# A four-block hybrid layer on one core: value rows repeated by TensorE into PSUM, and the update made there

## The chip, the cores and the metric

One core of a Trainium2 chip runs the program. The metric is the device time of one execution in microseconds (us). Names of engines: PE is TensorE (PEld its weight loads), DVE is VectorE, ACT is ScalarE, POOL is GpSimd, SP is SyncE, which only issues transfers here.

## The reference

2,048 tokens of 128 features pass through four sublayers, each with a layer norm in front and a residual behind: a gated delta attention (the one that the change touches), a mixture of 8 experts with top-2 routing, a random-feature attention, and the same mixture of experts again. The first sublayer, with 16 heads of 8 features, is:

```
q, k = l2norm(x @ Wq), l2norm(x @ Wk);  v = x @ Wv;  beta = sigmoid(x @ Wbeta)
def step(state, (qt, kt, vt, bt)):                    # over 2,048 tokens
    state = state * (1 - bt * kt kt^T) + bt * (vt kt^T)     # 8x8 per head
    return state, einsum('bhij,bhj->bhi', state, qt)
out = layernorm(outs) * ln_g + ln_b
out = (out * silu(x @ Wg)) @ Wout
```

The product with `kk` is element by element, so each of the 16 x 8 x 8 entries of the state is a scalar recurrence of its own along the tokens: state = decay * state + fresh, with decay = 1 - beta k_i k_j and fresh = beta v_i k_j.

## The kernel before, in words

Tokens are worked in four blocks of 512 (`NB`, index `c`). The recurrence has 1,024 scalar rows, which are 8 tiles of 128 partitions (`HD`, index `i`): partition (h, j) of tile i holds entry i, j of head h. So there are 32 steps, n = 8c + i, and each is one `tensor_tensor_scan` of 128 x 512 on DVE (L794), which starts from the last column of the same tile in the block before.

The operands of step n are made in these places. The k of a block (`kT`, L771) is stored to DRAM (`k_rows`, L301) and read back eight times, each time with row i of every head repeated over its 8 partitions (`spread`, L307) into `decay[:, i]`; v (`vT`, copied from PSUM by ACT, L524) goes through `v_rows` into `fresh[:, i]` in the same way (L299, L308). POOL multiplies `decay` by `bkT` = beta * k (`decay_product`, L424), ACT makes it 1 - decay (`one_minus`, L548), DVE multiplies `fresh` by `bkT` (`update`, L786) and scans. POOL then multiplies the state by q (`read_product`, L433), and PE sums over j (`sum_heads`).

Beside the steps, passes of the neighbouring blocks are spread over the loop: projections of q, k, v (`project_qk`, `project_v`), ACT's squares and raw copies (`square`), the sums of squares by PE (`sum_squares`), their square roots (`norms`), reciprocals (`clamp`), ACT's widening (`widen`) and PE's transposes (`expand`) that bring the reciprocal norms to the place of k and q, `unit_k` and `unit_q`; then, for the block behind, `copy_oT`, `turn_o`, `stats_o`, `ln_scale`, `normalise_o`, `turn_n`, `affine_nT`, `open_gates`, `out_a`, `add_a`, the next layer norm (`ln_rows`, `turn_rows`), and the routing of the first mixture (`logits`, `choose`, `rank`, `locate`, and the scatters of POOL, L442).

The order is written out by hand: each engine has a loop over n with `if i == ...` in it, and every instruction waits for semaphores that others raise. Each engine runs its own list strictly in order, so what stands behind a waiting instruction waits too. In the kernel before PE has no instruction that belongs to a single step except the head sums, so its loop can run ahead of DVE's. PSUM has eight banks of 512 float32 columns, `ps[:, 0..7, :]`: 0 to 2 hold q, k and v, 3 and 4 the sums of squares and the widened norms, 5 transposes, logits and ranks, 6 head sums, 7 transposes and the output product. Ahead of the loop come the layer norm of x, the projections of block 0, and for all four blocks beta (sigmoid) and the gate (silu).

The orders that the change touches, on PE and on DVE:

```
for n in range(NSTEP + HD + 2):      # DVE
    if n + 1 < NSTEP: update(n + 1)
    if n < NSTEP: scan(n)
    ...                              # choose, locate, stats_o, unit_k, open_gates, ... by i
```

Of the kernel before, what the change touches and what calls it, by code (L numbers as in the profile page):

```python
# [22 lines left out]
P = 128  # L23
# [3 lines left out]
H = 16  # L27
# [40 lines left out]
def program(nc, x, Wq, Wk, Wv, Wbeta, Wg, Wout, ln_g, ln_b, W_qkv, proj, W_out, b_out, w_g, c_fc, c_proj, out):  # L68
# [8 lines left out]
    with ctx:  # L77
# [51 lines left out]
        v_rows = nc.dram_tensor("v_rows", [NB, P, BK], F32).ap()  # L129

        with ExitStack() as a:
# [17 lines left out]
            vT = sb("vT", [P, 2, BK], F32, a)  # L149
# [3 lines left out]
            fresh = sb("fresh", [P, HD, BK], F32, a)  # L153
# [4 lines left out]
            nT = sb("nT", [P, BK], F32, a)  # L158
# [3 lines left out]
        with ExitStack() as mb:  # L162
# [110 lines left out]
        def _(sp):  # L273
# [23 lines left out]
            for c in range(NB):  # L297
                sp.wait_ge(v_ready, c + 1)
                sp.dma_start(v_rows[c], vT[:, c % 2, :]).then_inc(v_out, 16)  # L299
                sp.wait_ge(k_ready, c + 1)  # L300
                sp.dma_start(k_rows[c], kT[:, c % 2, :]).then_inc(k_out, 16)  # L301
                sp.wait_ge(v_out, 16 * (c + 1))
                sp.wait_ge(k_out, 16 * (c + 1))
                for i in range(HD):
# [3 lines left out]
                    sp.dma_start(fresh[:, i, :], spread(v_rows, c, i)).then_inc(fresh_in[i], 16)  # L308
# [68 lines left out]
        def _(pool):  # L377
# [10 lines left out]
            pool.memset(base_share[:], 0.0)  # L388
            pool.memset(later_tile[:], 1.0).then_inc(const_made, 1)
# [9 lines left out]
            for by_head in heads:  # L399
# [6 lines left out]
                               pattern=[[-1, P]], channel_multiplier=1)  # L406
            for e in range(NE):
# [41 lines left out]
            for n in range(NSTEP):  # L449
# [5 lines left out]
                if c >= 2 and i >= 2:  # L455
# [5 lines left out]
            read_product(NSTEP - 1)  # L461

# [40 lines left out]
        def _(act):  # L503
# [115 lines left out]
            ln_root(0, 0)  # L619
            turned_x(0, 5)  # L620
# [16 lines left out]
            one_minus(0)  # L637
            one_minus(1)
            for n in range(NSTEP + HD):
# [107 lines left out]
        def _(dve):  # L747
# [29 lines left out]
            def unit_q(c):  # L777
# [740 lines left out]
```

## Time and profile before

| | |
|---|---|
| median of 3 runs | 610.31 us (609.3 to 611.79) |
| profiled execution | 608.01 us |
| its span, first to last instruction | 606.1 us |
| mean granted TensorE clock | 0.766 of 2.4 GHz |
| busy: PE, DVE, ACT, POOL | 377.2, 330.3, 235.6, 268.1 us |

The profile is of one execution. Busy time is the sum of the durations of an engine's instructions, whether they ran freely or were held up while running. The granted clock is 1.00 at 2.4 GHz and 0.50 at 1.2 GHz; a value between is a mean over a stretch with both.

### The profile page before, as it was taken

The numbers are of one execution on the slowest core, as the hardware profiler recorded it, in microseconds if no ns is written. First come the engines' busy times: TensorE is split into PE (matmuls) and PEld (weight loads), VectorE is DVE, ScalarE is ACT, GpSimd is POOL, SyncE is SP. The second block draws the span as 40 slices with busy tenths as digits, with TensorE's granted clock in tenths as the row PEclk, the third lists the DMA queues.
The fourth block names the chain that finished last, engine by engine and source line by source line (L and its number), as shares of the span: only waits on it lengthen the run. The fifth ranks groups of instructions, "written<-read, shape, count | busy, mean of one in ns | idle before, by whom it ended". The sixth has DMA issues, their size and how long they took to land.

```text
span 606.1 us, 6487 instructions
## 1 busy us (share of the span) xinstructions
PE 377.2 (62%) x2106; PEld 247.0 (41%) x2106; DVE 330.3 (54%) x718; ACT 235.6 (39%) x343; POOL 268.1 (44%) x286
## 2 busy tenths in 40 slices
PE   4654628234154219999906899977776209999920
PEld 1422415112032107888803533333334207888720
DVE  4379797999984301231129699976776501111105
ACT  2472525223223203332303699877656301322300
POOL 3076886687875392564532200000523550545540
PEclk9796556765555559999956999996887557999965
DMA  4382959179102320212032433440000120122016
GB/s 113 100 229 78 315 180 340 67 256 316 38 26 44 149 74 27 76 52 68 33 105 74 104 93 96 100 145 1 32 14 27 35 77 24 52 74 73 28 57 176
DMA packets 46657, 60.14 MB, mean 99 GB/s; under 512 B 6816, under 2 KB 24864, under 8 KB 46624
## 3 DMA queue, kind: packets, MB, share of 16 engines
q1 hardware_dynamic: 41440, 51.09, 28.8%
q0 software_dynamic: 4608, 8.44, 4.1%
q8 instruction: 17, 0.28, 0.2%
q10 hardware_dynamic: 576, 0.21, 0.1%
q14 instruction: 16, 0.13, 0.1%
HBM read 34.46 MB, written 20.00 MB: 90 GB/s over the span
## 4 chain that ended last, share of the span: by engine, by line
PE 41%; DVE 25%; issue 7%; ACT 5%; DMA 4%; POOL 3%; SPq 1%; POOLq 0%; DVEq 0%; ACTq 0%
PE ps L1116 37%; DVE state L794 5%; DVE fresh L786 3%; DVE feat L1041 3%; POOL slots_x L442 2%; PE ps L1234 2%; ACT expo L698 2%; DVE ranked L845 2%; DVE xres L990 1%; DVE xres L985 1%; PE ps L1194 1%; DMA got<-chosen_y 1%; DMA xe<-slots_x 1%; ACT L698 1%; DMA slots_x<-rows_x,put_at 1%
## 5 line engine op out<-in xcount | busy, mean ns | idle before, releaser
L442 POOL DMA_INDIRECT slots_x<-rows_x,put_at x64 | 69.0, 1078 | 149.5 <-DVE put_at L874 130.6
L486 POOL DMA_INDIRECT chosen_y<-ye,y_to x80 | 79.3, 991 | 94.4 <-DVE ye L976 65.0
L610 ACT ACTIVATE hT<-ps 128x640 f32<-128x640 f32 x64 | 45.1, 704 | 139.4 <-PE ps L1116 133.8
L1041 DVE SCALAR_TENSOR_TENSOR feat<-expo,ps 128x1024 f32<-128x1024 f32 x64 | 76.8, 1218 | 11.5 <-ACT expo L698 11.1
L1116 PE MATMUL ps<-xeT,cfc_sb 128*128 128x320 f32 x256 | 75.7, 451 | 1.8 <-DVE xeT L958 1.8
L698 ACT ACTIVATE expo<-ps,minus_one 128x1024 f32<-128x1024 f32 x64 | 70.2, 1114 | 11.9 <-PE ps L1116 8.0
L1116 PE MATMUL ps<-cproj_sb,hT 128*128 128x128 f32 x640 | 74.6, 275 | 0.3
L1116 PEld LDWEIGHTS ps<-cproj_sb,hT 128*128 128x128 f32 x640 | 73.0, 192 | 0.9 <-issue 0.6
L958 DVE COPY xeT<-ps 128x640 f32<-128x640 f32 x16 | 13.2, 825 | 98.5 <-PE ps L1234 98.5
L424 POOL TENSOR_TENSOR decay<-decay,bkT 128x512 f32<-128x512 f32 x32 | 52.2, 1631 | 32.0 <-DMA decay<-k_rows 32.0
L794 DVE TENSOR_TENSOR_SCAN state<-decay,state,fresh 128x512 f32<-128x512 f32 x32 | 58.1, 1816 | 1.7 <-ACT decay L548 1.7
L1116 PEld LDWEIGHTS ps<-xeT,cfc_sb 128*128 128x128 f32 x256 | 47.7, 199 | 24.0 <-ACT hT L610 6.8
L433 POOL TENSOR_TENSOR read<-state,qT 128x512 f32<-128x512 f32 x32 | 44.6, 1394 | 20.6 <-DVE state L794 15.7
L976 DVE COPY ye<-ps 128x640 f32<-128x640 f32 x16 | 13.2, 825 | 63.4 <-PE ps L1116 63.4
L786 DVE TENSOR_TENSOR fresh<-fresh,bkT 128x512 f32<-128x512 f32 x32 | 34.9, 1091 | 7.8 <-DMA fresh<-v_rows 7.6
L1234 PE MATMUL ps<-ident,xe 128*128 128x128 f32 x80 | 12.5, 292 | 35.6 <-DMA xe<-slots_x 35.6
L570 ACT ACTIVATE std<-mv,eps_col 128x4 f32<-128x4 f32 x17 | 5.0, 296 | 70.3 <-DVE mv L828 26.9
L1116 PE MATMUL ps<-stk,pstk 97*128 97x512 f32 x64 | 24.2, 468 | 8.9 <-DVE feat L1041 8.0
L548 ACT ACTIVATE decay<-decay 128x512 f32<-128x512 f32 x32 | 19.8, 626 | 24.7 <-POOL decay L424 24.7
L1182 PE MATMUL ps<-ident,otok 128*128 128x128 f32 x16 | 4.5, 434 | 37.5 <-ACT otok L559 37.5
L1234 PEld LDWEIGHTS ps<-ident,xe 128*128 128x128 f32 x80 | 10.4, 151 | 38.6 <-issue 35.7
L1116 PE MATMUL ps<-feat,kvl 128*32 128x512 f32 x128 | 20.2, 707 | 8.3 <-DVE feat L1041 8.3
(188 smaller groups left out, 596.5 us busy)
## 6 DMA issues: line engine op xcount, KB each, us to landing
decay<-k_rows SPq DMA_DIRECT2D x32, 256.0 KB, 5.7
fresh<-v_rows SPq DMA_DIRECT2D x32, 256.0 KB, 6.8
stk<-part SPq DMA_DIRECT2D x96, 64.0 KB, 2.0
slots_x<-empty_rows SPq DMA_DIRECT2D x16, 322.5 KB, 8.0
xe<-slots_x SPq DMA_DIRECT2D x16, 322.5 KB
cfc_sb<-in_L_ffn_c_fc SPq DMA_DIRECT2D x2, 2048.0 KB, 8.7
got<-chosen_y SPq DMA_DIRECT2D x16, 256.0 KB, 4.7
chosen_y<-empty_rows SPq DMA_DIRECT2D x8, 256.0 KB
```

The lines of the kernel that those rows point to most:

```text
L424: pool.tensor_tensor(decay[:, i, :], decay[:, i, :], bkT[:, c % 2, :], ALU.mult).then_inc(product_ready, 1)
L433: pool.tensor_tensor(read[:, i, :], state[:, i, :], qT[:, c % 2, :], ALU.mult).then_inc(read_ready, 1)
L442: pool.indirect_dma_start(out=slots_x[k], out_offset=bass.IndirectOffsetOnAxis(ap=put_at[:, c, kk, t:t + 1], axis=0), in_=rows_x[:, kk * N ...
L486: pool.indirect_dma_start(out=chosen_y, out_offset=bass.IndirectOffsetOnAxis(ap=y_to[:, b, i:i + 1], axis=0), in_=ye[:, b, i * D:(i + 1) * ...
L548: act.activation(decay[:, n % HD, :], decay[:, n % HD, :], ACT.Identity, scale=-1.0, bias=1.0).then_inc(decay_ready, 1)
L610: act.activation(hT[:, b, f, :].rearrange("p (a n) -> p a n", a=2), ps[:, 2 + 2 * (f % 2):4 + 2 * (f % 2), 0:HALF], ACT.Gelu).then_inc(h_r ...
L698: act.activation(expo[:, g % 3, :], flat(ps[:, pair, :]), ACT.Exp, bias=minus_one[:]).then_inc(f_exp, 1)
L786: dve.tensor_tensor(fresh[:, i, :], fresh[:, i, :], bkT[:, c % 2, :], ALU.mult).then_inc(update_ready, 1)
L794: dve.tensor_tensor_scan(out=state[:, i, :], data0=decay[:, i, :], data1=fresh[:, i, :], initial=state[:, i, BK - 1:BK], op0=ALU.mult, op1 ...
L1041: dve.scalar_tensor_tensor(out=feat[:, g % 4, :], in0=expo[:, g % 3, :], scalar=1.0, in1=flat(ps[:, pair, :]), op0=ALU.min, op1=ALU.max).t ...
L1116: return pe.matmul(o, lhsT, rhs, start=start, stop=stop, **kw)
L1234: ins = pe.transpose(ps[:, i // TB, (i % TB) * P:(i % TB + 1) * P], xe[:, b, i, 0:D], ident[:])
```

## The change

The value rows no longer pass through DRAM. ACT copies v to `vhi` as float32r, DVE puts the rest into `vlo`, and for each step PE multiplies both by a selection matrix `sel[:, i]` (row i of each head, repeated over 8 partitions) into PSUM bank 3 or 4 by turns (`repeat_v`). `update` and the scan work on that bank. The sums of squares move to bank 7, the widened norms to banks 0 and 1. The scratch of `choose` in this stage, and the result of `affine_nT`, lie in bank 5. The gates and the betas of blocks 2 and 3 move from ahead of the loop into its first steps, and block 1's own preparation moves by one to two steps. On POOL the last two scatters of the loop go behind the last `read_product`.

```diff
-                sp.wait_ge(v_ready, c + 1)
-                sp.dma_start(v_rows[c], vT[:, c % 2, :]).then_inc(v_out, 16)
...
-                    sp.dma_start(fresh[:, i, :], spread(v_rows, c, i)).then_inc(fresh_in[i], 16)
...
+            pool.memset(sel_f[:], 0.0)
...
+            pool.affine_select(out=sel_f[:].rearrange("p i (h j) -> p i h j", j=HD),
...
-                if c >= 2 and i >= 2:
+                if c >= 2 and i >= 2 and n + 1 < NSTEP:
...
             read_product(NSTEP - 1)
+            for j in (6, 7):
+                scatter(0, 1, j)
...
-                copy(vT[:, c % 2, :], ps[:, 2, :]).then_inc(v_ready, 1)
+                copy(vhi[:, c % 2, :], ps[:, 2, :]).then_inc(vhi_ready, 1)
...
-                act.activation(nT[:], ps[:, 5, :], ACT.Identity, scale=lng[:], bias=lnb[:]).then_inc(nT_ready, 1)
+                act.activation(ps[:, 5, :], ps[:, 5, :], ACT.Identity, scale=lng[:], bias=lnb[:]).then_inc(nT_ready, 1)
...
+            ln_root(0, 0)
+            turned_x(0, 5)
             act.wait_ge(wall_in, 16 * 4)
...
-            turned_x(1, 7)
             norms(0)
+            turned_x(1, 5)
             widen(0)
             open_beta(0, 6)
-            turned_x(2, 5)
-            turned_x(3, 7)
-            for c in range(1, NB):
-                open_beta(c, (6, 5, 7)[c - 1])
+            open_beta(1, 6)
             act.wait_ge(w_in, 16 * 6)
-            for c in range(NB):
-                open_gate(c, (6, 5, 7, 6)[c])
...
                 if n + 2 < NSTEP:
                     one_minus(n + 2)
-                if i == 0 and c == 0:
+                if n == 0:
+                    turned_x(2, 5)
+                    turned_x(3, 6)
+                    open_beta(2, 5)
+                    open_beta(3, 6)
+                if n == 1:
+                    open_gate(0, 5)
+                    open_gate(1, 6)
+                if n == 2:
+                    open_gate(2, 5)
+                    open_gate(3, 6)
                     square(1)
+                if n == 3:
+                    copy_v(1)
+                    norms(1)
+                if n == 4:
+                    widen(1)
...
+            def low_v(c):
+                dve.wait_ge(vhi_ready, c + 1)
+                dve.tensor_tensor(vlo[:, c % 2, :], ps[:, 2, :], vhi[:, c % 2, :].bitcast(F32),
+                                  ALU.subtract).then_inc(vlo_ready, 1)
...
-                dve.tensor_tensor(fresh[:, i, :], fresh[:, i, :], bkT[:, c % 2, :], ALU.mult).then_inc(update_ready, 1)
+                c = n // HD
+                dve.wait_ge(vrep_ready, n + 1)
+                dve.tensor_tensor(ps[:, 3 + n % 2, :], ps[:, 3 + n % 2, :], bkT[:, c % 2, :],
+                                  ALU.mult).then_inc(update_ready, 1)
...
-                dve.tensor_tensor_scan(out=state[:, i, :], data0=decay[:, i, :], data1=fresh[:, i, :],
+                dve.tensor_tensor_scan(out=state[:, i, :], data0=decay[:, i, :], data1=ps[:, 3 + n % 2, :],
...
+            dve.wait_ge(sel_made, 1)
+            dve.tensor_copy(sel[:], sel_f[:]).then_inc(sel_made, 1)
+            low_v(0)
             clamp(0)
...
-                if i == 2 and c == 0:
+                if n == 4:
+                    low_v(1)
                     clamp(1)
+                if i == 1 and 1 <= c < NB - 1:
+                    low_v(c + 1)
...
-                if i == 3 + (c == 0) and c + 1 < NB:
+                if i == 3 + 2 * (c == 0) and c + 1 < NB:
                     unit_k(c + 1)
...
-                if i == 4 + (c == 0) and c + 1 < NB:
+                if i == 4 + 2 * (c == 0) and c + 1 < NB:
                     unit_q(c + 1)
...
             def project_qk(c):
                 if c:
-                    pe.wait_ge(raw_ready, c)
+                    pe.wait_ge(k_ready, c)
+                    pe.wait_ge(q_ready, c)
...
+            def repeat_v(n):
+                c, i = divmod(n, HD)
+                if i == 0:
+                    pe.wait_ge(vlo_ready, c + 1)
+                if n >= 2:
+                    pe.wait_ge(scan_done, n - 1)
+                mm(ps[:, 3 + n % 2, :], sel[:, i, :], vhi[:, c % 2, :], stop=False)
+                mm(ps[:, 3 + n % 2, :], sel[:, i, :], vlo[:, c % 2, :], start=False).then_inc(vrep_ready, 1)
...
             project_qk(0)
+            project_v(0)
+            sum_squares(0)
             pe.wait_ge(wbeta_ready, 1)
             project_beta(0, 6)
-            project_v(0)
-            turn_x(1, 7)
-            sum_squares(0)
+            turn_x(1, 5)
             expand(0)
+            pe.wait_ge(beta_ready, 1)
+            project_beta(1, 6)
+            pe.wait_ge(sel_made, 2)
+            repeat_v(0)
             turn_x(2, 5)
...
             for n in range(NSTEP + HD + 2):
                 c, i = divmod(n, HD)
-                if i == 0 and c == 0:
+                if n + 1 < NSTEP:
+                    repeat_v(n + 1)
+                if n == 0:
+                    project_beta(2, 5)
+                    project_beta(3, 6)
+                if n == 1:
+                    pe.wait_ge(w_in, 16 * 6)
+                    for j in range(2):
+                        pe.wait_ge(beta_ready, 3 + j)
+                        project_gate(j, 5 + j)
+                if n == 2:
+                    for j in range(2):
+                        pe.wait_ge(gate_ready, 1 + j)
+                        project_gate(2 + j, 5 + j)
                     project_qk(1)
+                if n == 3:
                     project_v(1)
+                    sum_squares(1)
+                if n == 4:
+                    expand(1)
...
                 if i == 1 and c >= 2:
-                    pe.wait_ge(logit_used, c - 1)
+                    pe.wait_ge(chosen_ready, c - 1)
                     rank(0, c - 2, 5)
```

## Rows read from the trace of the kernel before

**Rows 1.** Windows view: stretch, length; busy PE, PEld, DVE, ACT, POOL; clock, DMA share, GB/s.
```profile
71.00:108.00 37.00, 20.63 (x78) 12.41 (x74) 33.67 (x48) 14.51 (x28) 28.65 (x18) 0.60 0.84 274
108.00:146.00 38.00, 11.35 (x60) 6.17 (x52) 37.35 (x61) 9.90 (x21) 30.35 (x23) 0.63 0.61 194
146.00:183.00 37.00, 13.65 (x66) 6.94 (x61) 33.71 (x67) 9.68 (x20) 26.59 (x21) 0.50 0.24 70
```

**Rows 2.** Costliest groups of the page: line, engine, operation, busy us, mean ns, idle before.
```profile
L442 POOL DMA_INDIRECT slots_x<-rows_x,put_at x64 | 69.0, 1078 | 149.5 <-DVE put_at L874 130.6
...
L794 DVE TENSOR_TENSOR_SCAN state<-decay,state,fresh 128x512 f32<-128x512 f32 x32 | 58.1, 1816 | 1.7 <-ACT decay L548 1.7
...
L786 DVE TENSOR_TENSOR fresh<-fresh,bkT 128x512 f32<-128x512 f32 x32 | 34.9, 1091 | 7.8 <-DMA fresh<-v_rows 7.6
```

**Rows 3.** Timeline of DVE: start, duration, instruction, and idle time before it.
```profile
35.86 1.28 DVE L794 TENSOR_TENSOR_SCAN state<-decay,state,fresh 128x512 f32<-128x512 f32 x1 [1.70 <-ACT decay L548]
...
68.71 2.29 DVE L794 TENSOR_TENSOR_SCAN state<-decay,state,fresh 128x512 f32<-128x512 f32 x1
...
103.94 0.63 DVE L786 TENSOR_TENSOR fresh<-fresh,bkT 128x512 f32<-128x512 f32 x1
104.49 1.27 DVE L794 TENSOR_TENSOR_SCAN state<-decay,state,fresh 128x512 f32<-128x512 f32 x1
...
141.51 1.27 DVE L794 TENSOR_TENSOR_SCAN state<-decay,state,fresh 128x512 f32<-128x512 f32 x1
...
173.79 0.16 DVE L835 SCALAR_TENSOR_TENSOR shift<-mv,rstd 128x4 f32<-128x4 f32 x1
```

**Rows 4.** Timeline of all engines, DVE and POOL side by side in block 0.
```profile
39.84 2.18 POOL L424 TENSOR_TENSOR decay<-decay,bkT 128x512 f32<-128x512 f32 x1
40.88 1.68 DVE L786 TENSOR_TENSOR fresh<-fresh,bkT 128x512 f32<-128x512 f32 x1
...
41.98 1.71 POOL L433 TENSOR_TENSOR read<-state,qT 128x512 f32<-128x512 f32 x1
...
42.49 2.28 DVE L794 TENSOR_TENSOR_SCAN state<-decay,state,fresh 128x512 f32<-128x512 f32 x1
```

**Rows 5.** Timeline of all engines, ahead of the scanned stage.
```profile
7.01 0.31 ACT L504 ACTIVATE wbeta<-wall 128x128 f32<-128x128 f32 x1 [2.56 <-DMA wall<-in_L_attn_a_Wbeta]
...
21.43 0.69 DVE L771 TENSOR_TENSOR kT<-raw,ps 128x512 f32<-128x512 f32 x1 [1.41 <-PE ps L1157]
...
28.05 1.26 POOL L424 TENSOR_TENSOR decay<-decay,bkT 128x512 f32<-128x512 f32 x1 [22.39 <-DMA decay<-k_rows]
```

**Rows 6.** Source view of two DVE lines: duration in ns, min/median/max.
```profile
L771 DVE TENSOR_TENSOR kT<-raw,ps x4: 656/678/689, 21.4 to 121.2; 128x512 f32<-128x512 f32 x4
...
L845 DVE TENSOR_TENSOR ranked<-ranked,low_first x16: 191/192/5450, 106.1 to 480.0; 128x32 f32<-128x32 f32 x16
```

**Rows 7.** Timeline of PE, pairs of float32r matmuls in the attention that follows.
```profile
405.36 0.73 PE L1116 MATMUL ps<-stk,pstk 97*128 97x512 f32 x2 [0.41 <-DVE feat L1041]
...
420.89 1.20 PE L1116 MATMUL ps<-stk,pstk 97*128 97x512 f32 x2
```

**Rows 8.** Windows view, around the second of these pairs.
```profile
415.00:420.00 5.00, 4.50 (x18) 2.28 (x19) 3.65 (x7) 4.38 (x8) 0.00 (x0) 0.50 0.00 0
```

**Rows 9.** Timelines of ACT and PE, passes of block 1.
```profile
82.55 1.64 ACT L559 ACTIVATE otok<-ps,shift,rstd 128x128 f32<-128x128 f32 x4 [3.04 <-DVE shift L835]
...
84.24 1.12 PE L1182 MATMUL ps<-ident,otok 128*128 128x128 f32 x4 [10.16 <-ACT otok L559]
87.79 2.07 PE L1116 MATMUL ps<-wout,gated 128*128 128x128 f32 x8 [2.44 <-DVE gated L808]
...
99.03 3.44 PE L1116 MATMUL ps<-head_of,squares 128*128 128x16 f32 x16
```

**Rows 10.** Timeline of DVE, two more instructions.
```profile
52.52 0.66 DVE L771 TENSOR_TENSOR kT<-raw,ps 128x512 f32<-128x512 f32 x1
...
179.21 1.11 DVE L845 TENSOR_TENSOR ranked<-ranked,low_first 128x32 f32<-128x32 f32 x1
```

More of the change, by code:

```diff
@@ L148, in program @@
             kT = sb("kT", [P, 2, BK], F32, a)
-            vT = sb("vT", [P, 2, BK], F32, a)
+            vhi = sb("vhi", [P, 2, BK], F32R, a)
+            vlo = sb("vlo", [P, 2, BK], F32R, a)
+            sel_f = sb("sel_f", [P, HD, P], F32, a)
+            sel = sb("sel", [P, HD, P], F32R, a)
             qT = sb("qT", [P, 2, BK], F32, a)
@@ L770, in unit_k @@
                 dve.wait_ge(rep_mm, 2 * c + 1)
-                dve.tensor_tensor(kT[:, c % 2, :], raw[:, 1, :], ps[:, 3, :], ALU.mult).then_inc(k_ready, 1)
+                dve.tensor_tensor(kT[:, c % 2, :], raw[:, 1, :], ps[:, 0, :], ALU.mult).then_inc(k_ready, 1)
                 dve.wait_ge(k_ready, c + 1)
@@ L836, in ln_scale, with choose @@
                                          op0=ALU.mult, op1=ALU.mult).then_inc(ln_shift[n], 1)
-            def choose(k, c, lg):
+            def choose(k, c, lg, ranked, lg2):
                 wide = lambda ap: ap.unsqueeze(2).broadcast_to((P, TB, NE))
@@ L917, in _ @@
             update(0)
+            dve.wait_ge(ids_made, 1)
             begin_counts(0)
+            small = lambda n: ps[:, 5, 2 * P * (n > 0) + TB * NE * n:2 * P * (n > 0) + TB * NE * (n + 1)].rearrange(
+                "p (t e) -> p t e", e=NE)
             for n in range(NSTEP + HD + 2):
@@ L925, in _ @@
                 if i == 0 and c >= 2:
-                    choose(0, c - 2, ps[:, 5, 0:TB * NE].rearrange("p (t e) -> p t e", e=NE))
+                    choose(0, c - 2, small(0), small(1), small(2))
                 if i == 1 and c >= 2:
@@ L1095, in _ @@
                 elif n in ROUTE_AT:
-                    choose(1, ROUTE_AT[n], logits_in(pair_of(n).start + 1))
+                    choose(1, ROUTE_AT[n], logits_in(pair_of(n).start + 1), ranked[:], lg2[:])
                 elif n in RANK_AT:
@@ L1099, in _ @@
             divide(NB - 1, 1)
-            choose(1, NB - 2, logits_in(1))
+            choose(1, NB - 2, logits_in(1), ranked[:], lg2[:])
             add_b(NB - 1, 3)
@@ L1104, in _ @@
             ln_scale(4, NB - 1)
-            choose(1, NB - 1, logits_in(1))
+            choose(1, NB - 1, logits_in(1), ranked[:], lg2[:])
             locate(1, NB - 1, ranks_in(4))
@@ L1143, in sum_squares @@
                 pe.wait_ge(sq_ready, c + 1)
-                if c:
-                    pe.wait_ge(k_ready, c)
+                if c == 2:
+                    pe.wait_ge(wT_ready, 4)
+                if c >= 3:
+                    pe.wait_ge(xres_a, c - 2)
                 for t in range(TB):
                     for n in range(2):
-                        ins = mm(ps[:, 3, (2 * t + n) * H:(2 * t + n + 1) * H], squares[:, n, t * P:(t + 1) * P], head_of[:])
+                        ins = mm(ps[:, 7, (2 * t + n) * H:(2 * t + n + 1) * H], squares[:, n, t * P:(t + 1) * P], head_of[:])
                 ins.then_inc(sumsq_mm, 1)
             def expand(c):
-                for n, bank in ((1, 3), (0, 4)):
+                pe.wait_ge(raw_ready, c + 1)
+                for n, bank in ((1, 0), (0, 1)):
                     pe.wait_ge(wide_ready, 2 * c + 2 - n)
-                    if n == 0 and c:
-                        pe.wait_ge(q_ready, c)
                     for t in range(TB):
@@ L1297, in _ @@
                     expand(c + 1)
-                if i == 1 and c == 0:
-                    sum_squares(1)
                 if i == 1 and 1 <= c <= NB:
@@ L1306, in _ @@
                     if c == 1:
-                        pe.wait_ge(gate_ready, NB)
                         pe.wait_ge(wT_ready, 4)
                     turn_o(c - 1)
-                if i == 3 and c == 0:
-                    expand(1)
                 if i == 3 and c:
```

66 lines of the change are left out of this document (23 added, 43 removed).

## The prediction

> **What bounds the kernel now.** I read the page first, then the busy time by stage, then the timeline of each engine. The change touches only the scanned stage, from about 36 us to 183 us of a 606.1 us span. In the three windows that hold blocks 1 to 3, DVE is busy 33.67 of 37, 37.35 of 38 and 33.71 of 37 us, POOL 26.6 to 30.4 us, while PE is busy 0.30 to 0.56 of the time at a granted clock of 0.60, 0.63 and 0.50 [rows 1]. So DVE bounds these blocks.
>
> It is busy because it is slowed. 32 scans take 58.1 us, 1816 ns each, and 32 updates 34.9 us, 1091 ns each [rows 2]; alone a scan takes 1.27 us and an update 0.63 us [rows 3]. The difference is 58.1 - 32 x 1.27 = 17.5 us and 34.9 - 32 x 0.63 = 14.7 us. The timeline shows the cause: with a POOL product beside them an update takes 1.68 and a scan 2.28 us, and the POOL products 2.18 and 1.71 us instead of 1.26 [rows 4, 5]. The reader should see that all four have two SBUF inputs. kT<-raw,ps has one SBUF and one PSUM input, and its four executions, some beside POOL, all lie between 0.656 and 0.689 us [rows 6]. One tiny routing instruction with two SBUF inputs takes 0.191 us at best and 5.45 at worst [rows 6].
>
> **The change part by part.** I count from scan start to scan start: block 0 is 35.86 to 68.71, block 1 to 104.49, block 2 to 141.51, block 3 to the shift instruction at 173.79 [rows 3].
>
> *Contention removed.* Update gets PSUM in and out with one SBUF input, scan loses one SBUF input. By kT's row, I take 0.66 for an update and 1.28 for a scan beside POOL; PSUM as output and the scan's PSUM input are not shown, and bounds are the alone values 0.63 and 1.27 below and the stretched 1.68 and 2.28 above, where I take the row nearest in shape, kT's. POOL's products fall to 1.26. If nothing else came in, 32 us would go from DVE. The Trainium skill (SBUF — State Buffer, Who interferes with whom) says that a DVE instruction with at most one SBUF input doesn't contend with GpSimd. It would count the scan as free too, which no row here shows, since the scan also reads its starting value from SBUF.
>
> *A new wait in each step.* repeat_v(n+1) stands at the head of PE's loop n and waits for scan(n-1), because there are two banks; DVE's loop n begins with update(n+1), ahead of scan(n). So DVE's own next update waits for PE each time. The two float32r matmuls are not in the trace; the nearest are the pairs of 512-column fp32r matmuls of the key features, 0.73 us and, at a granted clock of 0.50, 1.20 us [rows 7, 8]. A bare step is scan 1.28 + pair + update 0.60 and about 0.1 of handing over: 2.7 us at 2.4 GHz and 3.2 us at 1.2 GHz, against 3.8 us for a fully stretched pair today (1.61 + 2.20, the starts in rows 4). That alone is a gain of 0.6 to 1.1 us a step.
>
> *What is queued in front of it.* PE works in order, and each repeat_v stands behind the PE work of the loop before. Today these passes wait with nobody behind them but later passes. Now DVE waits behind them:
> loop 3 of a block: turn_n waits for ACT's normalise (1.64), then 1.12, then the pair 1.20 [rows 7, 9]: 4.0 us behind ln_scale, of which kT and bkT cover 1.5: 2.5 us idle.
> loop 4: out_a 2.07 [rows 9] plus the pair, 3.3 us behind open_gates, unit_q covers 0.7: 2.6.
> loop 1: sum_heads, ACT's copy and turn_o, about 3.7 us beside scan and (blocks 2, 3) locate: 1 to 2.
> loop 0 in blocks 1 and 2: project_v and expand (eight transposes, 2 x 1.12): 1 to 2.
> loop 6: turn_rows behind ln_rows (four activations, as the 1.64 of rows 9), in block 1 also behind project_qk and square, since PE can no longer run ahead to start them: 3 to 5.
> loop 7 in block 1: sum_squares, 3.44 at the lower clock [rows 9], and logits before the next pair: 3.
>
> Walking the queues with these durations gives, scan start to scan start. Block 1 at the lower clock throughout: 4.4 + 4.9 + 3.2 + 6.4 + 5.9 + 3.6 + 8.0 + 6.5 = 42.9 us against 35.8. At the higher clock throughout, the pairs save 8 x 0.47 and the listed passes about half of their 16 us, 11.8 in all: 31.1. The dense stretches (expand to turn_o, out_a to project_qk) should run partly at 2.4 GHz; I take half of the difference, 37.1: **+1.3**. Block 2 has no project_qk, square, sum_squares or clamp; choose, thirteen small instructions that take an estimated 2.9 us unstretched, and locate lie under the PE waits: 4.8 + 4.1 + 3.2 + 6.4 + 5.9 + 3.7 + 5.6 + 3.1 = 36.8 at the lower clock, 35.6 mixed, against 37.0: **-1.4**. Block 3 drops project_v, expand and the unit steps: 29.2, mixed 28.5, to the shift, against 32.3: **-3.8**. Its choose also no longer catches stretches such as the 5.45 us.
>
> *Block 0.* turned_x(0) no longer waits behind the weights' arrival, which ACT met at 7.01 [rows 5]; ln_root could run at 5.2, so the front moves by 2.0 us, and sum_squares ahead of project_beta and turn_x(1) gives 0.6 more. kT(0) moves from 21.43 to 18.8, the first decay product from 28.05 to 25.45 [rows 5], and with the gates out of the way scan(0) starts at 25.45 + 1.26 + 0.63 = 27.4 instead of 35.86, 8.4 us sooner. The memset, select and copy that make sel lie before 13 us, where POOL's next product is at 25 us and DVE waits for ACT: nothing; uncovered, an estimated 1 us each. Then it is given back. repeat_v(2) stands behind project_beta(2) and (3), and these behind ACT's turned_x(2) and (3), themselves behind one_minus(2), 30.5: the pair ends about 35.4 and scan(1) starts at 36.1. repeat_v(3) comes behind two gates, repeat_v(4) behind two gates and project_qk(1) (42.4), repeat_v(5) behind sum_squares(1) (45.8), repeat_v(6) behind expand(1), which waits for clamp(1) in DVE's own queue (about 53). So scan(5) starts about 54 and kT(1) about 55.3, later than today's 52.52 [rows 10]. Rows of k go through DRAM as before: kT's end to product is 28.05 - 22.12 = 5.9 us [rows 5]. decay(8), one_minus(8), the wT copies, square(2), sum_squares(2), clamp(2) then follow one another on ACT, PE and DVE as today: scan(8) at 69.8 to 71.4 against 68.71. **+1.9**.
>
> *Removed DMAs.* 32 transfers of fresh and 4 stores go. Only decay transfers feed the first block now, but landing is no longer what the chain waits for after scan(0). Gain in the sum nothing; cover is the PE order above. Without that cover it is up to 1.6 us per early step.
>
> *Tail.* read_product(31) goes ahead of two scatters; but the DVE chain choose, locate, stats_o ends as late as the head sums, so only the routing instruction that took 1.11 instead of 0.19 [rows 6, 10] goes: **-0.9**. rank now waits for chosen_ready: 0.2 at most, behind choose.
>
> The PSUM operand of 64 DVE instructions: kT's median 0.678 against 0.63 of an update would be 0.05 x 64 = 3 us. I take nothing beyond the 0.66 used, since most of it overlaps in the starts. The Trainium skill (VectorE: DVE Perf Modes, The TRN2 errata) gives 120 cycles fixed for PSUM sources and 58 for SBUF; by that the 64 instructions would cost 4.1 us more and the sum would end on the other side of zero.
>
> **Sum.** +1.9 + 1.3 - 1.4 - 3.8 - 0.9 = -2.9 us. The profiled execution took 608.01 us (span 606.1), 2.3 below the median 610.31; -2.9 on it is 605.1, on the median **607.4 us**. Half a per cent, 3.05 us, is about what this kernel's measurement tells from no change.
>
> **Rivals.**
> A, as summed, PE's order eats what contention gives back: 607.4, own range 602 to 613, chance 0.45.
> B, the pairs keep TensorE at 2.4 GHz through most of the blocks. Block 1 -4, block 2 -4, block 3 -6, block 0 +1, tail -1: 596. For it: PE becomes busier. Against: the granted clock is 0.50 to 0.63 today [rows 1], and gaps of 1 to 2 us remain. 0.20.
> C, the other side: TensorE stays at 1.2 GHz through the blocks. +2.7 + 7.1 - 0.2 - 3.1 - 0.9, with 0.2 per step of handing over in the bound steps of block 1: about +7, 617. It decides from a mean clock of about 0.6 in block 1 downward. 0.17.
> D, the scan stays stretched by POOL because its starting value comes from SBUF: 1.0 us on half of the scans, +16: 621. Against: nothing in the rows, which is why it has 0.07.
> E, the waits are shorter than walked and POOL bounds: 32 x 2 x 1.23 = 79 us of products and 16 scatters of 1.08 plus gaps [rows 2], about 100 us instead of 138: 575. For it: all 32 us of stretch. Against: the PE order. 0.06.
> F, the fixed cost of PSUM operands, 3 us by kT's row: 610.4, no change. 0.05. This is the rule of VectorE: DVE Perf Modes in the Trainium skill.
>
> Faster by over 0.5%: half of A, B, E: 0.48. Within: the middle of A and F: 0.26. Slower: the rest of A, C, D: 0.26. The range 594 to 618 holds A, C and most of B, leaves out E and D.
>
> **What would show it.** Right: scans at 1.28 with POOL products at 1.26 throughout; before update, DVE idle ended by PE in nearly every step; scan(0) at 27 to 28 and scan(8) at 69 to 72; a long idle ahead of update(2). Wrong: kT(1) before 52 us; DVE idle before updates under 0.5 us a step (E); scans of 2.28 (D); granted clock over 0.85 or at 0.50 in all blocks (B, C).

## The result, and the profile after

The changed kernel takes 620.07 us (median of 4, 617.86 to 621.44), the kernel before 609.8 (608.9 to 611.79) beside it: 1.016 times as long, 95% interval 1.0121 to 1.02. It is slower by 10 us; 607.4, and at most 618, was forecast. The profiled execution took 620.1 us, its span 618.0 against 606.1.

What was to come off came off. The costliest groups of the page after:

```profile
L442 POOL DMA_INDIRECT slots_x<-rows_x,put_at x64 | 63.0, 985 | 152.1 <-DVE put_at L886 127.6
...
L433 POOL TENSOR_TENSOR read<-state,qT 128x512 f32<-128x512 f32 x32 | 40.7, 1272 | 45.4 <-DVE state L806 39.8
...
L424 POOL TENSOR_TENSOR decay<-decay,bkT 128x512 f32<-128x512 f32 x32 | 40.5, 1267 | 34.4 <-DMA decay<-k_rows 34.4
...
L797 DVE TENSOR_TENSOR ps<-ps,bkT 128x512 f32<-128x512 f32 x32 | 22.2, 694 | 44.7 <-PE ps L1137 44.5
L806 DVE TENSOR_TENSOR_SCAN state<-decay,state,ps 128x512 f32<-128x512 f32 x32 | 40.6, 1270 | 1.6 <-ACT decay L550 1.6
...
L1137 PE MATMUL ps<-vhi,sel 128*128 128x512 f32 x32 | 23.1, 722 | 15.4 <-DVE state L806 15.3
```

Against [rows 2], a scan fell from 1816 to 1270 ns and an update from 1091 to 694: 58.1 + 34.9 - 40.6 - 22.2 = 30.2 us of VectorE gone. The last column of the update's row says where they went: 44.7 us of idle time of VectorE ahead of the updates, 44.5 of it ended by TensorE. Windows of blocks 1 to 3, columns as in [rows 1]:

```profile
74.00:111.00 37.00, 23.00 (x91) 14.87 (x91) 25.92 (x46) 14.97 (x30) 19.96 (x16) 0.68 0.47 149
111.00:150.00 39.00, 19.03 (x78) 10.34 (x76) 28.74 (x63) 11.12 (x23) 25.95 (x23) 0.63 0.37 113
150.00:184.00 34.00, 14.63 (x52) 6.81 (x52) 26.36 (x58) 6.20 (x13) 21.92 (x19) 0.60 0.31 91
```

No engine is full in them: DVE is down to 70 to 78%, TensorE at 43 to 62% at a granted clock of 0.60 to 0.68, a little above that of before. When every engine has time to spare, the stage is bound by what waits for what; e1 below shows how much of that is order.

The timeline of DVE after, answering to [rows 3, 10]:

```profile
5.81 2.91 DVE L764 TENSOR_SCALAR xn<-xres,mv,rstd 128x128 f32<-128x128 f32 x4
...
29.77 1.28 DVE L806 TENSOR_TENSOR_SCAN state<-decay,state,ps 128x512 f32<-128x512 f32 x1 [1.62 <-ACT decay L550]
37.19 0.70 DVE L797 TENSOR_TENSOR ps<-ps,bkT 128x512 f32<-128x512 f32 x1 [6.14 <-PE ps L1137]
37.80 1.27 DVE L806 TENSOR_TENSOR_SCAN state<-decay,state,ps 128x512 f32<-128x512 f32 x1
...
56.68 0.66 DVE L777 TENSOR_TENSOR kT<-raw,ps 128x512 f32<-128x512 f32 x1
```

The same stations for all kernels, read from the same view (starts in us, of the profiled execution; e1 to e10 are the experiments below; shift is the last `shift<-mv,rstd` of the stage, behind scan(30)):

| kernel | scan(0) | kT(1) | scan(8) | scan(16) | scan(24) | shift | span | median, ratio to before |
|---|---|---|---|---|---|---|---|---|
| before | 35.86 | 52.52 | 68.71 | 104.49 | 141.51 | 173.79 | 606.1 | |
| after | 29.77 | 56.68 | 73.98 | 110.80 | 150.34 | 182.52 | 618.0 | 620.07, 1.016 |
| e1 | 29.34 | 50.49 | 66.52 | 102.71 | 136.56 | 169.81 | 602.8 | 604.26, 0.9913 |
| e2 | 28.94 | 54.93 | 71.89 | 108.04 | 143.06 | 172.00 | 605.5 | 608.13, 0.9984 |
| e3 | 34.84 | 49.64 | 65.64 | 102.71 | 142.23 | 174.40 | 610.1 | 612.21, 1.0043 |
| e4 | 30.83 | 52.59 | 68.81 | 105.88 | 142.89 | 175.15 | 607.7 | 610.52, 1.002 |
| e5 | 33.51 | 49.06 | 65.15 | 101.39 | 134.03 | 167.06 | 601.9 | 603.85, 0.9914 |
| e6 | 27.18 | 54.12 | 71.10 | 108.53 | 148.07 | 180.27 | 617.7 | 617.54, 1.0137 |
| e7 | 28.73 | 49.73 | 65.66 | 99.71 | 132.33 | 162.48 | 595.7 | 599.05, 0.9858 |
| e8 | 32.00 | 47.55 | 63.88 | 98.07 | 130.39 | 160.56 | 592.8 | 596.31, 0.9815 |
| e9 | 27.54 | 48.64 | 57.25 | 92.11 | 128.94 | 159.09 | 594.2 | 594.87, 0.9761 |
| e10 | 26.76 | 48.22 | 57.28 | 90.38 | 125.80 | 153.63 | 589.8 | 591.61, 0.9712 |

The changed kernel against the one before, in us: block 0 +5.3 by scan(8), block 1 +1.0, block 2 +2.5, block 3 -0.1, and +3.2 behind the shift.

### The profile page after: what moved, and what is told of

It reads as the page before. It is cut to its first block, busy times and chain, and to the rows that moved or that the text cites. A ratio compares the mean times of both kernels' runs of the same rounds, so it can differ in the third digit from the quotient of the medians.

```text
span 618.0 us, 6592 instructions
## 1 busy us (share of the span) xinstructions
PE 402.2 (65%) x2170; PEld 260.4 (42%) x2170; DVE 303.9 (49%) x723; ACT 235.0 (38%) x343; POOL 249.6 (40%) x288
## 4 chain that ended last, share of the span: by engine, by line
PE 51%; DVE 22%; issue 9%; DMA 6%; ACT 6%; POOL 4%; SPq 1%; POOLq 0%; DVEq 0%; ACTq 0%
PE ps L1137 45%; DVE state L806 4%; DVE feat L1062 3%; POOL slots_x L442 2%; DVE shift L847 2%; PE ps L1268 2%; DMA decay<-k_rows 1%; PE ps L1228 1%; ACT expo L704 1%; DVE xres L1011 1%; DVE xres L1006 1%; DMA got<-chosen_y 1%; ACT otok L561 1%; DMA xe<-slots_x 1%; DVE stats L837 1%
## 5 line engine op out<-in xcount | busy, mean ns | idle before, releaser
L442 POOL DMA_INDIRECT slots_x<-rows_x,put_at x64 | 63.0, 985 | 152.1 <-DVE put_at L886 127.6
L979 DVE COPY xeT<-ps 128x640 f32<-128x640 f32 x16 | 13.2, 824 | 99.1 <-PE ps L1268 99.1
L433 POOL TENSOR_TENSOR read<-state,qT 128x512 f32<-128x512 f32 x32 | 40.7, 1272 | 45.4 <-DVE state L806 39.8
L424 POOL TENSOR_TENSOR decay<-decay,bkT 128x512 f32<-128x512 f32 x32 | 40.5, 1267 | 34.4 <-DMA decay<-k_rows 34.4
L997 DVE COPY ye<-ps 128x640 f32<-128x640 f32 x16 | 13.2, 824 | 64.0 <-PE ps L1137 64.0
L797 DVE TENSOR_TENSOR ps<-ps,bkT 128x512 f32<-128x512 f32 x32 | 22.2, 694 | 44.7 <-PE ps L1137 44.5
L806 DVE TENSOR_TENSOR_SCAN state<-decay,state,ps 128x512 f32<-128x512 f32 x32 | 40.6, 1270 | 1.6 <-ACT decay L550 1.6
L1137 PE MATMUL ps<-vhi,sel 128*128 128x512 f32 x32 | 23.1, 722 | 15.4 <-DVE state L806 15.3
L1137 PE MATMUL ps<-feat,kvl 128*32 128x512 f32 x128 | 21.9, 763 | 7.2 <-DVE feat L1062 7.1
```

Of the source, the lines that this page charges most:

```text
L424: pool.tensor_tensor(decay[:, i, :], decay[:, i, :], bkT[:, c % 2, :], ALU.mult).then_inc(product_ready, 1)
L433: pool.tensor_tensor(read[:, i, :], state[:, i, :], qT[:, c % 2, :], ALU.mult).then_inc(read_ready, 1)
L442: pool.indirect_dma_start(out=slots_x[k], out_offset=bass.IndirectOffsetOnAxis(ap=put_at[:, c, kk, t:t + 1], axis=0), in_=rows_x[:, kk * N ...
L797: dve.tensor_tensor(ps[:, 3 + n % 2, :], ps[:, 3 + n % 2, :], bkT[:, c % 2, :], ALU.mult).then_inc(update_ready, 1)
L806: dve.tensor_tensor_scan(out=state[:, i, :], data0=decay[:, i, :], data1=ps[:, 3 + n % 2, :], initial=state[:, i, BK - 1:BK], op0=ALU.mult ...
L1137: return pe.matmul(o, lhsT, rhs, start=start, stop=stop, **kw)
```

## The experiments

e2 leaves one matmul out, so that its values are coarser; all others compute everything. The diffs are cut to the lines that matter and are against the changed kernel unless said otherwise.

### e1: the repeat one loop earlier

```diff
+            repeat_v(1)
             for n in range(NSTEP + HD + 2):
-                if n + 1 < NSTEP:
-                    repeat_v(n + 1)
+                if n + 2 < NSTEP:
+                    repeat_v(n + 2)
```

> The changed kernel with one edit: PE issues repeat_v one loop earlier, so the passes of loop n stand behind the repeat for step n+2, instead of ahead of it. Nothing is left out. Theory Q (PE's queue order costs the change its gain): DVE's idle before updates, 44.5 us in 21 waits, falls below 25 us, and the time to 600 to 608 us against 620 for the changed kernel. Theory L (the pair of matmuls is itself too slow, whatever its place): idle stays above 38 us and the time within 3 us of 620. Against both: sum_squares at loop 7 now stands behind a repeat that waits for the last scan of the block, which may cost up to 3.4 us in blocks 0 and 1.

604.26 us (5 runs), ratio 0.9913 (0.9881 to 0.9945): 16 us off by moving one line. The waits of DVE in the stage, first after (29 to 185 us), then e1 (29 to 186); columns: us in total, times, longest:

```profile
DVE ps L797 <- PE ps L1137: 44.0, 20, 6.1
DVE rnorm L771 <- ACT norm L530: 6.8, 2, 5.1
```

```profile
DVE rnorm L771 <- ACT norm L530: 16.2, 3, 7.6
DVE ps L797 <- PE ps L1137: 13.5, 13, 2.8
DVE table L878 <- PE ps L1137: 6.5, 3, 3.7
DVE top L855 <- PE ps L1137: 3.6, 1, 3.6
```

Of 44.0 us behind the repeats 30.5 are gone, and half of them come back as other waits: 9.4 more for the norms and 5.9 for the ranking (`table`), whose TensorE work now stands behind a repeat that waits for a scan. The wait of `top` and the last 0.6 of `table` lie behind e1's shift; the changed kernel has the same wait of `top`, 3.62, at 188.84, outside its window. Block 0 is 7.0 us shorter, block 2 5.7, block 1 0.6, and block 3 is 1.1 longer. The clock does not explain it: in blocks 1 to 3 it is 0.74, 0.60 and 0.51, against 0.68, 0.63 and 0.60 in the changed kernel, higher only in the block that hardly moved. In block 0 it is 0.78 against 0.73, so part of the 7.0 may be the clock's.

### e2: one matmul in each repeat

```diff
-                mm(ps[:, 3 + n % 2, :], sel[:, i, :], vhi[:, c % 2, :], stop=False)
-                mm(ps[:, 3 + n % 2, :], sel[:, i, :], vlo[:, c % 2, :], start=False).then_inc(vrep_ready, 1)
+                mm(ps[:, 3 + n % 2, :], sel[:, i, :], vhi[:, c % 2, :]).then_inc(vrep_ready, 1)
```

> The changed kernel with only the vhi matmul in repeat_v, in the old order; the low part of v is left out of the computation. A step whose update waits for PE gets 0.40 to 0.63 us sooner. Theory Q: 20 such waits, so 8 to 11 us less, 609 to 612, and the waits behind turn_n and out_a (2.0 to 3.7 us each) keep 1.5 us or more. Theory L: at least 15 us less, 605 or lower.

608.13 (10 runs), ratio 0.9984 (0.995 to 1.0017): 12 us off after's. But the waits behind TensorE fall only from 44.0 to 37.1. Blocks 0 and 1 are 1.3 and 0.7 shorter, blocks 2 and 3 4.5 and 3.2. There the small `shift<-mv,rstd` takes 0.16 (122.34, 157.97) instead of 3.00 and 3.01, and in block 2 a bkT takes 3.10 in its place: what a shorter repeat shifts in time may count for more than its length. With 608.13 neither reading of the expectation came true: it lies between Q's 609 to 612 and L's 605. So the length of the pair has a price too, beside its place: 2.0 us in blocks 0 and 1, where the shifts kept their 1.25. How much of the rest of the 12 us is length and how much is the stretch that moved, this run does not separate; e7 shows what the stretch is worth by itself.

### e3 and e4: the gates' place, with and without the repeats

e3 puts the gates and betas ahead of the loop and block 1's preparation back to before's steps; e4 is the kernel before with the changed kernel's order of them, its earlier front included. Of e3's edit, the lines of ACT ahead of the loop; TensorE's list changes likewise:

```diff
+            turned_x(2, 5)
+            turned_x(3, 6)
+            open_beta(2, 5)
+            open_beta(3, 6)
+            for c in range(NB):
+                open_gate(c, 5 + c % 2)
```

> The changed kernel with the gates and the betas of blocks 2 and 3 ahead of the loop again, and block 1's preparation in the loops where the kernel before had it. Theory G (moving the gates in costs block 0 its gain): scan(0) starts at 35 to 37 instead of 29.8, but scan(8) at 65 to 69 instead of 74.0, and the time is 612 to 617. Rival (the placement of the gates is neutral, block 0 is bound by the order of the PE passes of block 1 and 2): scan(8) at 72 to 76, the time within 2 us of 620.

> The kernel before, with value rows through DRAM, but with the gates moved into block 0 and block 1's preparation later, in the order of the changed kernel. Theory G: the chain kT(1), decay transfer, squares, clamp(2) starts later, so 2 to 5 us slower than before, 612 to 615. Rival (gates in the block fill idle time of ACT and PE, and only the repeats make them costly): scan(8) at 63 to 66 instead of 68.7 and 4 to 6 us faster, 604 to 606.

e3: 612.21 (10 runs), 1.0043 (1.0017 to 1.0069), 8 us off after's, all in block 0 (scan(8) 8.3 earlier, the later blocks equal to after's within 0.3). e4: 610.52 (10 runs), 1.002 (0.9991 to 1.0049): scan(0) 5.0 earlier and scan(8) where it was. Neither of e4's two forecasts came true (612 to 615, 604 to 606): what the early scan(0) wins is given back by scan(8). So the moved gates, with block 1's preparation and the earlier front, cost nothing on balance where no repeat is queued behind them; in the changed kernel the gates and that preparation cost 8. The two are not separated.

### e5: both orders

The edits of e1 and e3 together.

> Changed kernel with both orders of the earlier runs: each repeat issued one loop earlier on TensorE, and the gates and the betas of blocks 2 and 3 ahead of the loop with block 1's preparation where the kernel before has it. Theory Q+G (the two costs are separate: head-of-line waiting of the repeats 16 us, gates inside block 0 costing because they sit on the same queue 8 us): part of the 8 us was already recovered by the order, because the gates' passes then delay a repeat that has a loop of slack, so 598 to 602; scan(8) at about 64 to 65. Rival (the gates' cost was only through the queue, so the order took it all): 603 to 606, no better than the 604.3 of the order alone. Rival (gates ahead of the loop delay scan(0) by 5 us as they did, and nothing gives it back): 607 or more.

603.85 (7 runs), 0.9914 (0.9886 to 0.9943), the same as e1. The first rival (603 to 606) holds: the price of the gates was their place in the queue, and e1 had already taken it off.

### e6: the choice scratch filled later

```diff
+            pool.wait_ge(ln_out[0], TB)
+            pool.memset(sel_f[:], 0.0).then_inc(sel_made, 1)
+            pool.wait_ge(sel_made, 1)
+            pool.affine_select(out=sel_f[:]...
```

These lines stand behind the last memset of the setup; their old places are empty.

> Changed kernel, only the choice scratch is filled later: its memset (0.94) and its select (2.01) on GpSimd stand behind everything else of the setup and behind norm_x(0). Theory F (norm_x(0) took 2.91 instead of 1.11 because GpSimd filled the scratch beside it, which cost the 1.8 us that the earlier beginning had won): norm_x(0) back at 1.1, the first transposes on TensorE 1.8 earlier, kT(0) and scan(0) 1.5 to 2 us earlier, 618 us. Rival (something else, the weights' transfer, holds the front): norm_x(0) at 1.1 but the projection still at 10.2 and scan(0) at 29.8, 620 us. Rival (the stretch has another cause): norm_x(0) stays near 2.9.

After, then e6, all engines at the start:

```profile
4.73 2.01 POOL L403 TENSOR_SCALAR_AFFINE_SELECT sel_f<-sel_f 128x1024 f32<-128x1024 f32 x1
...
5.81 2.91 DVE L764 TENSOR_SCALAR xn<-xres,mv,rstd 128x128 f32<-128x128 f32 x4
...
7.98 1.42 PE L1142 MATMUL ps<-ident,xn 128*128 128x128 f32 x4 [7.98 <-DVE xn L764]
```

```profile
5.85 1.12 DVE L766 TENSOR_SCALAR xn<-xres,mv,rstd 128x128 f32<-128x128 f32 x4
6.34 1.15 PE L1144 MATMUL ps<-ident,xn 128*128 128x128 f32 x4 [6.34 <-DVE xn L766]
...
18.56 0.69 DVE L779 TENSOR_TENSOR kT<-raw,ps 128x512 f32<-128x512 f32 x1 [1.79 <-PE ps L1182]
...
25.16 1.26 POOL L426 TENSOR_TENSOR decay<-decay,bkT 128x512 f32<-128x512 f32 x1 [15.03 <-DMA decay<-k_rows]
...
27.18 1.28 DVE L808 TENSOR_TENSOR_SCAN state<-decay,state,ps 128x512 f32<-128x512 f32 x1 [1.69 <-ACT decay L552]
```

617.54 (4 runs), 1.0137 (1.0102 to 1.0172): 2.5 less than the changed kernel, a difference inside the intervals of both, but the stations move by 2.2 to 2.9, where 1.5 to 2 was expected. The span of the profiled execution is only 0.3 shorter: some 2.5 us come back in the last stretch, from the first `feat` to the last mixed row, where the code is the same (257.1 against 254.6). The front itself is clear: norm_x(0) takes 1.12 instead of 2.91, and the scratch beside it had cost what the early start won.

### e7: the shift with one SBUF input

e1's order, and:

```diff
+                other = ps[:, 5, 0:TB] if n < 4 else rstd[:, tt]
+                if n < 4:
+                    dve.reciprocal(other, std[:, tt])
                 dve.reciprocal(rstd[:, tt], std[:, tt]).then_inc(ln_rstd[n], 1)
...
-                dve.scalar_tensor_tensor(out=shift[:, tt], in0=mv[:, tt, 0], scalar=-1.0, in1=rstd[:, tt],
+                dve.scalar_tensor_tensor(out=shift[:, tt], in0=mv[:, tt, 0], scalar=-1.0, in1=other,
```

> Repeats one loop earlier, and the small operation that makes the shift (mean times -rstd, 128x4) takes rstd from a copy in PSUM, made by a second reciprocal of 0.15, so that it has one SBUF input instead of two. Theory S (the 3.00 us of it at 118.1 and 156.6 are two GpSimd products that it waits for, since it holds two SBUF inputs): it takes 0.2 everywhere, VectorE wins 2.8 twice and 1.1 several times, 604.3 - 5 = 599, at least 601. Rival (its length is the wait for std or for a queue that the record counts in): stays near 3 us, 604.5. Rival (it shortens, but the update then waits for TensorE or the decays' transfers instead): 0.2 each and 603 to 605.

599.05 (4 runs), 0.9858 (0.9817 to 0.9899), 5.2 less than e1 (its slowest run, 601.84, lies below e1's fastest, 603.92); in the profiled executions blocks 1, 2 and 3 are 2.1, 1.2 and 3.1 shorter. Block 2 in e1, then in e7:

```profile
118.11 3.01 DVE L847 SCALAR_TENSOR_TENSOR shift<-mv,rstd 128x4 f32<-128x4 f32 x1
...
118.59 1.28 POOL L433 TENSOR_TENSOR read<-state,qT 128x512 f32<-128x512 f32 x1
...
119.82 1.27 POOL L424 TENSOR_TENSOR decay<-decay,bkT 128x512 f32<-128x512 f32 x1
121.04 0.68 DVE L777 TENSOR_TENSOR kT<-raw,ps 128x512 f32<-128x512 f32 x1
121.15 1.63 ACT L561 ACTIVATE otok<-ps,shift,rstd 128x128 f32<-128x128 f32 x4 [4.43 <-DVE shift L847]
```

```profile
115.16 0.16 DVE L850 SCALAR_TENSOR_TENSOR shift<-mv,ps 128x4 f32<-128x4 f32 x1
115.23 0.68 DVE L777 TENSOR_TENSOR kT<-raw,ps 128x512 f32<-128x512 f32 x1
115.35 1.63 ACT L561 ACTIVATE otok<-ps,shift,rstd 128x128 f32<-128x128 f32 x4 [1.28 <-DVE shift L850]
...
115.94 1.29 POOL L433 TENSOR_TENSOR read<-state,qT 128x512 f32<-128x512 f32 x1
115.95 3.06 DVE L780 TENSOR_TENSOR bkT<-kT,beta 128x512 f32<-128x512 f32 x1
```

A four-column operation lasts 3.01 us: it ends at 121.12, 0.03 behind the second of two POOL products that follow each other without a gap (and behind a scatter that was running when it began). In e7 it lasts 0.16, and the next operation with two SBUF inputs, bkT, takes the stretch. That still wins, since kT and the otok chain (ACT, turn_n, the next repeat) are already under way. This is what the first reading had forecast (at least 601).

### e8: everything, with the squares ahead

Both orders, e6, e7, and for blocks 2 and 3 `square` and `norms` ahead of `one_minus` on ACT, `sum_squares` ahead of the repeat on PE.

> All of it together: both orders, choice scratch filled later, the shift with one SBUF input, and for blocks 2 and 3 the squares and norms ahead of the decay's one_minus on ScalarE and the sums of squares ahead of the repeat on TensorE (the clamp of these blocks waited 7.6 us twice). Theory (order on the queues is the whole bound in the scanned stage, each wait removed is VectorE time won): 604.3 - 4 (gates) - 1.5 (front) - 5 (shift) - 5 (clamp) = 589, at least below 596. Rival (GpSimd or the transfers of the decays become the bound: GpSimd is busy 83 us of a stage of 140, and a decay arrives 19 us after its kT): no better than 598. Rival (the ranking after the stage takes back what the scans win): scans end 12 to 15 earlier, time above 598.

596.31 (4 runs), 0.9815 (0.9773 to 0.9858). Expected was less than 596, and the rivals said over 598. Against e7 only the stretch up to scan(8) moved (kT(1) 2.2 earlier, scan(8) 1.8), by e6's edit and e3's together; blocks 1 to 3 take 34.2, 32.3 and 30.2 against 34.1, 32.6 and 30.2. DVE still waits up to 7.2 us at once for the norms. In all these waits fell from 15.5 to 11.2 us, and those of the updates rose from 13.2 to 18.3: the squares' new place won nothing.

### e9 and e10: the clamp behind the scan, then the ranking

e9 is e7 with e6's edit and, in DVE's list:

```diff
+                if i == 0 and 1 <= c < NB - 1:
+                    clamp(c + 1)
...
-                if i == 7 and c + 2 < NB:
-                    clamp(c + 2)
```

e10 adds to e9 a copy of the tile starts in PSUM for the running count (`upto`), and `rank` ahead of the repeat in loop 1 of a block.

> Repeats one loop earlier, shift with one SBUF input, choice scratch filled later, gates inside block 0 as the change has them, and the clamps of blocks 2 and 3 on VectorE one loop later, behind the first scan of the next block, so that VectorE does not wait for the norms (7.6 and 7.6 us of waiting in the run with the order alone). Theory: 599.05 - 2 (front) - some 10 of the 15 us of waiting = 587, at least below 593. Rival (TensorE's expand now waits for the clamp with the next repeat behind it, so the wait moves to the update): 594 to 597, with the waits of the updates behind TensorE up by 5 or more from 13.2.

> The run before it in this call, with two more edits: the running count of the chosen experts takes its tile starts from a copy in PSUM (one SBUF input instead of two; it took 3.7 to 4.1 us in block 3 beside GpSimd, 0.3 without), and the ranking's eight small matmuls stand ahead of the repeat that waits for the scan, since locate waited 2.2 and 3.7 us for them. Theory: 3.4 + 5 us less than that run, at least 5 less. Rival (the next operation with two SBUF inputs, or the next wait, takes the time over): within 2.5 of it.

e9: 594.87 (4 runs), 0.9761 (0.9712 to 0.981). scan(8) comes at 57.25, 8.4 ahead of e7; but scan(24) is only 3.4 ahead, and the waits of the updates rise from 13.2 to 18.2: the rival's forecast, in the time too (594 to 597). e10: 591.61 (4 runs), 0.9712 (0.9675 to 0.9748), 3.3 less than e9 where at least 5 was expected. The waits of locate went (7.4 to 0.6), and the running count took 0.29 instead of 3.68, but in block 3:

```profile
129.39 1.27 POOL L426 TENSOR_TENSOR decay<-decay,bkT 128x512 f32<-128x512 f32 x1
129.55 0.23 DVE L871 COPY ps<-later_tile 128x64 f32<-128x64 f32 x1
129.81 0.29 DVE L872 TENSOR_TENSOR_SCAN upto<-ps,chosen 128x64 bf16<-128x64 f32 x1
130.02 3.10 DVE L876 TENSOR_TENSOR gap<-top 128x4 f32<-128x4 f32 x1
...
133.04 0.69 DVE L799 TENSOR_TENSOR ps<-ps,bkT 128x512 f32<-128x512 f32 x1
```

the next operation with two SBUF inputs, the four-column gap, took 3.10. Even so e10 is 5.5 us ahead of e9 at the last shift. The rest is lost behind it: `stats` then waits 2.31 us for TensorE's `turn_o`, for which it did not wait there in e9, and the first expert's copy of xeT comes only 2.7 us earlier. Both kernels of the case are slower: before by 18 us, the changed one by 28. No run separates the two edits of e10.

## Why the prediction was wrong

**Right: contention removed.** Scans 1.27 (1.28 said), updates 0.694 (0.66), POOL products 1.27 (1.26) throughout; against [rows 4] no scan, update or product is stretched. Rival D is out. The 0.034 too little on the update is 1.1 us over 32.

**Right: a new wait in each step, and its cause.** A pair takes 0.73 (139.69 to 140.42, granted clock 1.00) or 1.20 (136.52 to 137.72, 0.50), as in [rows 7]. 20 of 32 updates wait for TensorE, 44 us in all, as the queues said; e1 shows that 30 of them are order and not TensorE's work. **Block 1** was forecast at +1.3 and came at +1.0. Its steps in the walk were 4.4, 4.9, 3.2, 6.4, 5.9, 3.6, 8.0, 6.5 at the lower clock; measured 2.7, 2.9, 2.9, 7.0, 5.5, 3.5, 6.3, 6.0. That the sum came right is partly luck. The block is 6.1 us under the walk at the lower clock; 3.7 of them lie in its first two steps, whose updates waited 0.8 and 0.4 us where the walk had 1 to 2 for each, while 5.8 had been taken off as half of what the higher clock would give.

**The step that failed: the walk of blocks 2 and 3 under "What is queued in front of it".** Its sums, 35.6 and 28.5, were 39.5 and 32.2 (terms -1.4 and -3.8, measured +2.5 and -0.1). That is 7.6 of the 14.8 us by which the difference of the spans (+11.9) missed the forecast (-2.9); block 0 has 3.4 of the rest and the tail 4.1. The steps of block 2 were walked as 4.8, 4.1, 3.2, 6.4, 5.9, 3.7, 5.6, 3.1 and measured

```profile
110.80 1.27 DVE L806 TENSOR_TENSOR_SCAN state<-decay,state,ps 128x512 f32<-128x512 f32 x1
...
124.11 1.27 DVE L806 TENSOR_TENSOR_SCAN state<-decay,state,ps 128x512 f32<-128x512 f32 x1
...
125.48 3.00 DVE L847 SCALAR_TENSOR_TENSOR shift<-mv,rstd 128x4 f32<-128x4 f32 x1
...
130.19 1.12 PE L1216 MATMUL ps<-ident,otok 128*128 128x128 f32 x4 [6.73 <-ACT otok L561]
...
132.27 0.70 DVE L797 TENSOR_TENSOR ps<-ps,bkT 128x512 f32<-128x512 f32 x1 [2.46 <-PE ps L1137]
...
132.88 1.27 DVE L806 TENSOR_TENSOR_SCAN state<-decay,state,ps 128x512 f32<-128x512 f32 x1
```

as 4.7, 5.5, 3.2, 8.8, 5.5, 3.5, 5.2, 3.2. The one from 124.11 to 132.88 is 2.4 over: the walk gave ln_scale its free duration. The prediction had seen such stretches of small operations, and counted them as gone with choose's move to PSUM. They are not gone, they hit the ones that still have two SBUF inputs. The 3.00 of the shift stands ahead of otok, turn_n, the repeat and the update, so it counts in full: the idle time behind it is still 2.46 us, where 2.5 was said. Block 3 has the same (a step of 8.7, with 3.01 at 164.80; the prediction shows no steps for block 3). e7, on top of e1's order, takes this out and wins 5.2 us. The second step, 5.5 for 4.1, has no TensorE wait in it at all: DVE is busy with locate, and in it `dropped` takes 0.78 and `put_at` 1.18 instead of 0.17 each, stretched as before; the walk had laid locate under a TensorE wait. And 1.2 us of the miss in block 2, 0.7 in block 3, had been taken off for the higher clock: without that the walk said 36.8 and 29.2.

The Trainium skill (SBUF — State Buffer, Who interferes with whom) has the rule that a DVE instruction with two SBUF inputs contends with a GpSimd instruction that reads SBUF. The traces agree and show more: DVE was passed over at the boundary of two back-to-back POOL products too (e1, 118.11 to 121.12), and of three (e10, 130.02 to 133.12). For instructions with at most one SBUF input the same section makes an exception of the 2-port perf modes, which the prediction's sentence leaves out; `dropped` and norm_x(0) have one SBUF input and were stretched here (0.78, 2.91), and whether they ran in such a mode no trace shows.

**Failed: block 0, +5.3 against +1.9.** Of the 3.4, 2.4 are the front: scan(0) at 29.77 and not 27.4. The filling of the choice scratch was costed at nothing, "before 13 us", with only POOL's next product and DVE's later wait as cover. The select alone took 2.01, twice the 1 us of the estimate. The cover was missing at 5.81, where norm_x(0) took 2.91 instead of the 1.11 that the same operation takes at 12.62. With e6 kT(0), the first product and scan(0) come at 18.56, 25.16 and 27.18; the prediction had 18.8, 25.45 and 27.4. From there the walk of the queues was close: scan(1) 8.0 behind scan(0) (8.7 said), scan(5) 25.7 (26.6), kT(1) 26.9 (27.9). kT(1) to scan(8) then took 17.3 us where some 15 was said; 5.1 of it is DVE waiting for the norms of block 2 at the end of loop 7.

**Half right: A.** It was the mechanism, mis-sized. **C** gave 617, near the truth, for another reason, a granted clock of 0.50; it was 0.60 to 0.68. **D** gave 621 for a stretch of the scans that is not there; its 16 us were added to the profiled execution, on the median they make 623.4. B and E are out (E's 38 us less than today are 572 by its own numbers, not 575). F is too: the updates are 0.064 above [rows 3]'s 0.63, 2.0 us over 32 of which the sum held 1.0, and the scans with a PSUM input stayed at 1.27. Even the 0.064 is not shown to be PSUM's: in the kernel before, updates with all operands in SBUF took 0.63 at 103.94 and 0.69 at 115.03. Of the 4.1 us that VectorE: DVE Perf Modes (The TRN2 errata) in the Trainium skill would add, none is there on the scans and at most 2.0 on the updates.

**Tail, +3.2 against -0.9.** The last shift took 1.51 instead of 0.16. The first expert's copy of xeT comes 52.9 us behind the start of that shift, 51.9 before; the first `feat` 121.7 behind the copy, 120.7 before; the last mixed row 254.6 behind that, 253.4 before. The routing instruction took 0.20 as forecast, and behind scan(31) VectorE waits 3.62 us for TensorE's logits where it had waited 1.89. The last two stretches are the same code, and the last one lies between 253.0 and 257.1 in the twelve kernels of the case. That scatter is not explained, so some 2 us of the +3.2 may be no effect of the change.

## What to carry to other kernels

When work moves to an idle engine that runs its list in order, write down what stands ahead of it in that list: with 32 pairs of 0.7 to 1.2 us VectorE waited 44 us, and issuing them one loop earlier gave 16 us back. Where no engine is full, look at the order first. Operations that keep two SBUF inputs beside a busy GpSimd must be walked at the length of what may run there, however small they are, and each one made free hands the stretch on: free those that start a chain, and let it fall on one that nobody waits for.

## What was not expected of the hardware

- A VectorE operation of 4 to 64 columns with two SBUF inputs can last to the end of the run of adjacent GpSimd products beside it: 3.01 (e1), 3.10 (e10) and 3.68 us (e9) instead of 0.16, 0.13 and 0.29.
- A `tensor_scalar` from SBUF to SBUF (norm_x, four of 128 columns) took 2.91 us beside GpSimd's select and memsets, 1.12 in e6 with GpSimd idle.
- The scan's starting value in SBUF costs no contention: all 32 scans after lie between 1262 and 1279 ns, with GpSimd busy 67% of block 2.
